# First gate of a two-layer mixture-of-experts kernel: turned input ahead of the rest, row means out of the gate's products, squares on ScalarE

## The reference

```python
x = x + 0.5 * ffn(layernorm(x))      # mixture of 8 experts, top 2 of each row
x = x + attention(layernorm(x))      # 16 heads, causal
x = x + 0.5 * ffn(layernorm(x))      # the same experts again
```

```python
m = mean(x, -1); v = var(x, -1); xn = (x - m) / sqrt(v + 1e-5)
logits = xn @ gate_weight.T                      # (4096, 8)
top_w, top_i = top_k(softmax(logits), 2)         # two experts and weights per row
primary = experts that are the first choice of some row
# experts that are nobody's first choice are rerouted by the similarity matrix
y[e] = (silu(g) * u) @ down[e].T,  g, u = split(xn @ gate_up[e].T)
out  = sum over the two experts of weight * y[e]
```

## Time and profile before

| | |
|---|---|
| time, median of 3 runs (lowest, highest) | 1196.34 us (1195.28, 1199.88) |
| the profiled execution: time, span | 1202.0 us, 1200.3 us |
| the first gate in its span | about 3 to 97.8 us |
| DVE busy over the span | 767.0 us (64%) |
| PE busy over the span | 993.4 us (83%) |
| ACT, POOL busy over the span | 675.0 us (56%), 508.3 us (42%) |

### The profile page before, as it was taken

How to read it: one execution, slowest core, us unless ns; L and a number is a source line. 1 busy time by engine, 2 the same in 40 slices (tenths; PEclk the granted TensorE clock), 3 DMA queues, 4 the chain that set the end, 5 groups by cost and what they waited for, 6 DMA issues and landing times. The chain is left out here.

```text
span 1200.3 us, 25180 instructions
## 1 busy us (share of the span) xinstructions
PE 993.4 (83%) x9046; PEld 722.6 (60%) x9046; DVE 767.0 (64%) x1557; ACT 675.0 (56%) x1595; POOL 508.3 (42%) x692
## 2 busy tenths in 40 slices
PE   5226999999789967999999999999887299999930
PEld 1125788787778854555555555555546178888830
DVE  3995444444377637888888888888617844444437
ACT  2733445444357522777787877878737545555410
POOL 1535667675455540222232323323210067777720
PEclk9757999999579985999999999999969689999975
DMA  8723555553447554345464553544219423333349
GB/s 305 229 97 98 191 196 202 198 182 136 154 135 249 178 157 90 73 106 123 98 148 104 113 119 95 122 103 102 57 45 344 162 84 105 103 102 106 98 140 315
DMA packets 100582, 172.94 MB, mean 144 GB/s; under 512 B 16240, under 2 KB 64368, under 8 KB 100464
## 3 DMA queue, kind: packets, MB, share of 16 engines
q1 hardware_dynamic: 86640, 133.57, 38.9%
q0 software_dynamic: 13824, 37.77, 9.2%
HBM read 101.55 MB, written 69.47 MB: 142 GB/s over the span
## 5 line engine op out<-in xcount | busy, mean ns | idle before, releaser
L1814 ACT ACTIVATE spare<-h_psS 128x512 f32<-128x512 f32 x576 | 306.6, 601 | 92.8 <-PE h_psS L1724 90.5
L1842 DVE TENSOR_REDUCE h_part<-h_psM 128x2 f32<-128x1024 f32 (+3 forms) x256 | 249.1, 1015 | 11.5 <-PE h_psM L1703 10.9
L1877 POOL TENSOR_SCALAR_AFFINE_SELECT spare<-spare 128x256 f32<-128x256 f32 x256 | 99.5, 407 | 303.7 <-ACT spare L1814 303.7
L886 PE MATMUL m_psG<-wgu,m_x_hi 128*128 x576 | 195.0, 420 | 1.2 <-DVE m_x_lo L960 1.2
L864 POOL DMA_INDIRECT ys<-m_y,m_slot_u x144 | 142.3, 988 | 78.4 <-ACT m_y L951 53.5
L1751 PE MATMUL h_psO<-spare,a_VP 128*17 128x256 f32 (+3 forms) x3072 | 167.0, 337 | 8.9 <-ACT spare L1805 8.7
L1703 PE MATMUL h_psM<-h_KT,h_QT 48*128 48x512 f32 (+3 forms) x768 | 146.2, 423 | 22.5 <-DMA h_QT<-a_QD 14.8
L1724 PE MATMUL h_psS<-h_QT,h_KT 49*128 49x512 f32 (+3 forms) x768 | 159.2, 407 | 3.0 <-ACT spare L1814 2.3
L858 POOL DMA_INDIRECT m_xg<-xn,m_slot_u x140 | 135.7, 969 | 47.8 <-issue 22.3
L970 DVE TENSOR_TENSOR m_h<-m_act_g,m_psG 128x256 f32<-128x256 f32 x144 | 60.6, 421 | 136.1 <-ACT m_act_g L944 136.1
L886 PE MATMUL m_psY<-wdn,m_h_hi 128*128 x576 | 128.5, 304 | 10.8 <-issue 6.5
(11 more groups left out here) (230 smaller groups left out, 1570.4 us busy)
## 6 DMA issues: line engine op xcount, KB each, us to landing
xn<-spare SPq DMA_DIRECT2D x16, 512.0 KB, 5.8
wg_d<-wgu SPq DMA_DIRECT2D x16, 512.0 KB
p_yg<-ys SPq DMA_DIRECT2D x16, 512.0 KB, 5.5
a_KD<-spare SPq DMA_DIRECT2D x32, 256.0 KB, 3.0
h_KT<-a_KD SPq DMA_DIRECT2D x64, 128.0 KB
h_QT<-a_QD SPq DMA_DIRECT2D x64, 128.0 KB
a_OD<-spare SPq DMA_DIRECT2D x128, 64.0 KB, 2.5
wgu<-wg_d SPq DMA_DIRECT2D x16, 512.0 KB, 10.5
```

Of the source, the lines that this page charges most:

```text
L886: m = pe.matmul(out, s[:, c, :], ww[:, bass.ds(at + c * width, width)], start=(n == 0), stop=(n == 3 * CC - 1))
L1814: act.activation(prob[k % NP][:, h, :], psS[x % NS][:, :], ACT.Exp).then_inc(s_read, 1)
L1842: m = dve.tensor_reduce(out, psM[k % NM][:, :, at:at + n], AX.X, ALU.max, negate=True)
L1877: m = pool.affine_select(block, block, [[0, 2], [1, P]], ALU.is_ge, 0.0, 0, -1)
```

## The change

1. SP issues all eight `turned(h)` first, then weights and rows by turns, then the similarity matrix, and all stores last, in the order 0, 1, 4, 2, 5, 6, 3, 7.
2. The gate product uses all M = 10 columns of `middle`; columns 8 and 9 hold -1/256, so that column 8 gives minus the mean of each row. `measure` goes. `means(q)` copies that column into SBUF, and ACT gets `square(h)`: four activations that square X plus the negative mean, with the sum over the row as second result. `deviate` reads these sums.
3. Normalised rows: groups 0 to 3 by ACT (two buffers), 4 to 7 by DVE (two buffers). Before it was 0 to 5 and 6 to 7.
4. `low_places` reads a new f32 ramp `iota_f` in place of the bf16 one, and that of batch 0 is cut in halves around `choices(1)`.
5. The lists of ACT and DVE are put in a new order. `ranks(0)` goes from behind group 6 to behind group 7.

```diff
-    W, RA, RB, RT = 4, 3, 1, 4
+    W, RA, RB, RT, M = 4, 2, 2, 4, sh.M
-    BY_ACT, BY_DVE = tuple(range(NH - 2)), (NH - 2, NH - 1)
+    BY_ACT, BY_DVE = tuple(range(NH // 2)), tuple(range(NH // 2, NH))
@@ SP
                 for h in range(NH):
-                    load(h)
                     turned(h)
...
+                for e in (0, 1): weights(e)
+                load(0); load(1)
+                for e in (2, 3): weights(e)
+                load(2); load(3); weights(4); load(4); load(5); weights(5)
+                load(6); load(7); weights(6); weights(7)
                 route.similarities(sp, sim_d)
+                for h in (0, 1, 4, 2, 5, 6, 3, 7):
+                    store(h)
@@ PE
-                        m = pe.matmul(psL[h % 2][0:E, :], middle[:, c, 0:E], xT[h % RT][:, c, :], ...
+                        m = pe.matmul(psL[h % 2][0:M, :], middle[:, c, :], xT[h % RT][:, c, :], ...
-                    if h == NH - 2:
+                    if h == NH - 1:
                         route.ranks(pe, 0)
@@ ACT
+                def square(h):
+                    act.wait_ge(x_in[h], 16)
+                    act.wait_ge(mean_done, route.batch_of(W * h) + 1)
+                    act.wait_ge(centred, 1)
+                    for t in range(W * h, W * h + W):
+                        if t >= 2:
+                            act.wait_ge(squared, t - 1)
+                        act.activation(psM[:, t % 2 * C:t % 2 * C + C], X[:, t, :], ACT.Square, bias=mean[:, t:t + 1],
+                                       accum_out=squares[:, t:t + 1]).then_inc(squared, 1)
...
                 # the new list, shortened to its calls
+                across(0..7); high(0); high(1); square(0); square(1); high(2); high(3); square(2); square(3)
+                deviate(0); high(4); partitions(0..2); normal(0); normal(1); square(4); square(5); high(5)
+                partitions(3); square(6); square(7); deviate(1); high(6); partitions(4); normal(2)
+                partitions(5); high(7); partitions(6); normal(3); partitions(7); exponentials
@@ POOL
+                pool.iota(iota_f[:, :], [[1, P]], 0, 0, ...).then_inc(iota_done, 1)
@@ DVE
-                        dve.bn_stats(stats[:, t, :], X[:, t, :]).then_inc(stat_done, 1)
-                        dve.bn_aggr(mv[:, t, :], stats[:, t, :]).then_inc(var_done, 1)
-                    dve.scalar_tensor_tensor(shift[:, at], mv[:, at, 0], -1.0, rstd[:, at], ...
+                    dve.tensor_tensor(shift[:, at], mean[:, at], rstd[:, at], ALU.mult).then_inc(rs_done, 1)
+                def means(q):
+                    dve.wait_ge(lg_done, route.FROM[q + 1] // W)
+                    dve.tensor_copy(mean[:, route.tiles(q)], scores(q)[:, :, E]).then_inc(mean_done, 1)
...
+                means(0); choices(0); place(0); low_places(0, half 0); means(1); choices(1)
+                low_places(0, half 1); begins; place(1); shift; block_places(0..2); invert(0)
+                low_places(1); block_places(3..5); invert(1); block_places(6); normal(4)
+                block_places(7); normal(5); normal(6); normal(7); open_gap; similar; weights; slots; experts
```

More of the change, by code:

```diff
@@ L605, in _ @@
                 for h in range(NH):
[L606 removed]
                     turned(h)
[L608 to L611, removed]
[L612 to L622 removed]
+                for e in (0, 1):
+                    weights(e)
+                load(0)
+                load(1)
+                for e in (2, 3):
+                    weights(e)
+                load(2)
+                load(3)
+                weights(4)
+                load(4)
+                load(5)
+                weights(5)
+                load(6)
+                load(7)
+                weights(6)
+                weights(7)
+                route.similarities(sp, sim_d)
+                for h in (0, 1, 4, 2, 5, 6, 3, 7):
+                    store(h)
                 for j in range(RA):
@@ L771, in _ @@
                                          gate_w[:, :, :], ALU.mult, ALU.add).then_inc(centred, 1)
-                for h in range(5):
-                    measure(h)
+                means(0)
                 choices(0)
-                invert(0)
-                for h in range(5, NH):
-                    measure(h)
                 route.place(dve, T, 0)
+                dve.wait_ge(iota_done, 1)
+                route.low_places(dve, 0, 0, iota_f)
+                means(1)
                 choices(1)
-                invert(1)
-                normal(BY_DVE[0])
-                route.open_gap(dve, T, rstd[:, :])
-                route.low_places(dve, 0)
+                route.low_places(dve, 0, 1, iota_f)
                 route.begins(dve, T)
@@ L788, in _ @@
                     route.block_places(dve, i)
-                normal(BY_DVE[1])
-                route.low_places(dve, 1)
-                for i in range(3, route.CH):
+                invert(0)
+                route.low_places(dve, 1, None, iota_f)
+                for i in range(3, 6):
                     route.block_places(dve, i)
+                invert(1)
+                route.block_places(dve, 6)
+                normal(4)
+                route.block_places(dve, 7)
+                for h in range(5, NH):
+                    normal(h)
+                route.open_gap(dve, T, rstd[:, :])
+                route.similar(dve, T)
                 route.weights(dve, T)
-                route.similar(dve, T)
                 route.slots(dve, T)
```

89 lines of the change are left out of this document (49 added, 40 removed).

## The result

The changed kernel takes 1205.06 us (median of 20 runs, 1199.24 to 1210.72). The kernel before, run beside it, takes 1200.20 us (median of 20, 1195.28 to 1205.89; the three runs shown ahead of the prediction are among them). The ratio is 1.0035, 95% interval 1.0018 to 1.0051: slower by 0.35% by this ratio, by 4.9 us between the two medians. That is within the half a per cent that the prediction called no change; only the very end of the interval reaches it. Part of the closeness of the total (1.5 us) is therefore luck: two errors of opposite sign. The profiled execution of the changed kernel took 1206.9 us, with a span of 1205.2.

A forecast was written before the change was run, and what follows sets the result against it. DVE, held by POOL's subtractions, was taken to bound the first gate; with ACT's late list and DVE's tail its end moves from 92.4 to 99.7 us, so 1196.34 + 7.3 = 1203.6 us, range 1190 to 1208.5.

The forecast's parts named there:

- The path: First gate: DVE under POOL to the first block matrix at 62.2 us, ACT to 79.05, then DVE to 99.7.
- the held ramp: First half of low_places(0), 16 f32-ramp instructions: held by POOL at 1.2 us each, 0.22 in quiet.
- ACT's wait: At ACT's first partition: from 45.8 us it waits 16 us for DVE's first block matrix at 62.2.
- DVE's wait for the second deviation: After low_places(1): DVE, done long before, waits for ACT's deviate(1), which ends at 79.05 us.
- a store ahead of `normal(7)`: Late on DVE: normal(7) waits until group 5 is stored, 0.15 + 2.9 us, to 92.2.
- the tail: From the second deviation's end on ACT, 79.05 us, through DVE's last matrices, normalisations and slot list, to 99.7.
- D: End of the slot list on DVE, closing the first gate: 92.4 us before, forecast 99.7, +7.3.
- The front: Loads, scores, first choices: DVE picks batch 0 from 21.2 to 25.9 us, group 7 scored 27.3, DVE on at 28.6.
- `place(0)`: DVE's step from 28.6 to 35.0 us: five of seven instructions each end with a POOL instruction; 1.7 without POOL.
- The unheld ramp: Rival, chance 0.25: POOL doesn't hold the f32 ramp, first half takes 4.3 us, D 96.0, total 1199.9.
- Only long runs are held: Rival, chance 0.2: place(0)'s small instructions slip past POOL in 1.8 us; D 86.6, -5.8, total 1190.5.
- The late stores: Rival, chance 0.1 with other length: group 5's store takes 7.8 us or queues; D 104.6, total 1208.5.

The follow-up runs named there:

- squares ahead: Changed kernel with ACT's squares of groups 4 to 7 and the second deviation ahead of its first partition; D 94.67 us against 96.9.
- tail filled: Changed kernel with open_gap and similar moved ahead of the normalisations of group 7, into DVE's store wait; D 93.99 us against 96.9.
- bf16 ramp: Changed kernel with the old bf16 ramp as source of all places, nothing else; D 94.23 us against 96.9.
- choices first: Changed kernel with means(1) and choices(1) ahead of the first half of batch 0's places; D 94.11 us against 96.9.
- rows as before: Changed kernel with six groups normalised by ACT, two by DVE, open_gap and similar ahead of the last group; D 91.24 us against 96.9.
- the last version: Changed kernel with the single edits combined, first of two orders (all squares and second deviation ahead of partitions); D 81.1 us, ratio 0.9919 to the kernel before.

## Why the prediction was right

**The steps that held.** The path, the held ramp, ACT's wait (14.99 us, 16 predicted), DVE's wait for the second deviation, a store ahead of `normal(7)`, and above all the tail: from the end of the second deviation's ACT instruction to D 99.7 - 79.05 = 20.65 us were predicted, and 96.90 - 76.24 = 20.66 measured. Its parts agree as well: `normal(4)` 4.1 predicted and 4.15 measured, `normal(5)` 4.05 and about 4.2, from its end to `normal(7)` 3.1 and about 3.1. The front was right to 0.7 us: choices(0) from 20.9 to 25.4 (21.2 to 25.9), group 7 scored at 26.8 (27.3), DVE going on at 27.99 (28.6). All of this follows the working by which the timelines of before were continued.

**The terms that were mis-sized.** D came 2.8 us earlier than predicted (96.9, not 99.7):

| term | predicted | measured | effect on D |
|---|---|---|---|
| DVE goes on after the ranks | 28.6 | 27.99 | -0.6 |
| `place(0)` | 6.4 | 4.0 | -2.4 |
| first half of the matrices | 13.7 | 14.4 | +0.7 |
| `means(1)`, `choices(1)` | 4.8 | 4.9 | +0.1 |
| second half | 3.5 | 3.2 | -0.3 |
| to ACT's first partition | 5.2 | 5.25 | 0 |
| ACT to the second deviation's end | 16.85 | 16.5 | -0.4 |
| tail | 20.65 | 20.66 | 0 |

One term is far larger than the others: `place(0)`. The working had each of its five one-source instructions end with an instruction of POOL. The trace shows two passing at 0.17 us each: L204 behind L203 and L206 behind L205, pairs in which the second doesn't wait for the first. POOL's next instruction starts at the same moment as L204 (30.56). This is no fixed property of the code. With squares ahead the same seven instructions took 6.4 us, L204 and L206 costing 1.30 us each, though POOL stood as in the changed kernel to 0.02 us (L203 starts 1.34 us after its first subtraction in both, POOL's third subtraction 2.47 and 2.45 us after it). In the four other kernels of that kind (tail filled, bf16 ramp, choices first, rows as before) L204 took 0.17 us. It looks like a tie at the change of turns that went the other way once in six. Timeline of DVE, squares ahead:

```profile
28.64 0.53 DVE L202 CAST m_rank_i<-m_rank 128x32 int32<-128x32 f32 x1
29.19 1.20 DVE L203 TENSOR_SCALAR m_hi_i<-m_rank_i 128x32 int32<-128x32 int32 x1
30.31 1.30 DVE L204 TENSOR_SCALAR m_lo_i<-m_rank_i 128x32 int32<-128x32 int32 x1
31.64 1.19 DVE L205 CAST m_hi<-m_hi_i 128x32 f32<-128x32 int32 x1
32.75 1.30 DVE L206 CAST m_lo<-m_lo_i 128x32 f32<-128x32 int32 x1
34.09 13.39 DVE L216 TENSOR_SCALAR spare<-m_iota_f,m_lo 128x128 bf16<-128x128 f32 x16
```

So the working gave the upper of two values that one and the same list of instructions can show, 4.0 and 6.4. The 2.4 us don't reach D whole, though. When `place(0)` takes them, POOL has that much less left to do behind it: in the one trace that shows it, with squares ahead, the first half took 13.39 us instead of 14.38, and `choices(1)` with `means(1)` 4.6 instead of 5.0. From DVE's going on to the second half it is 24.3 us there, 23.3 in the changed kernel, and 24.9 in the working (53.5 - 28.6). The rows -2.4, +0.7 and +0.1 of the table thus belong together: of their sum of -1.6 us the two ways of `place(0)` are 1.0, and 0.6 are the working's own. With the held `place(0)` D would have come near 97.9, a shift of some +5.5 by this estimate, which is still within half a per cent. The side with the largest of the three chances, "slower by more than half a per cent" at 0.43, didn't come because of that 1.0 us and of several small terms of the same sign (-0.6, -0.6, -0.3, -0.4); "same" had been given 0.42. The range of 1190 to 1208.5 was wide: the kernel before lies in it too.

**The rivals.** The unheld ramp gave +3.6 us, nearer in size than the forecast, and is false all the same: the f32 ramp cost 14.38 us beside POOL and 3.23 without it, and the same 16 in bf16 cost 12.06. A forecast can be nearer for the wrong reason; the row that was named in advance (0.27 or about 1.2 us each between 35 and 48) tells them apart. It showed 1.21 each at first (four in the 4.85 us from 32.01) and 0.21 in POOL's pause (five in the 1.06 us from 42.88), so that the mean of 0.90 is a mixture of the two. "Only long runs are held" asked for a `place(0)` under 2 us, and it took 4.0. The late stores didn't come: `normal(7)` waited 1.80 us.

The Trainium skill, SBUF — State Buffer, section Who interferes with whom, has a Vector instruction with one source through both ports and a GpSimd instruction shut each other out for the other's whole length, by the number of ports alone. The mixed form bears this out (1.21 us each held, 0.20 in quiet), as the int32 instructions of `place` do. In these traces the holding isn't confined to instructions with one source: block matrices, with two, took 1.8 us instead of 0.75 with the squares ahead.

**What stays open.** Why the two instructions pass in one execution and not in another isn't settled: the starts agree to 0.02 us, where the rows resolve 0.01, and no run repeats one kernel's trace to count how often. The tie is a guess; the six traces show only the two outcomes. The gains of the single edits weren't tried in every pairing either, so that the 11.3 us of the last version can't be shared out among them. And of the 1.5 us that POOL costs more than before, no run says which part comes from where POOL's instructions now lie and which from such ties.

## What to carry to other kernels

Where POOL's instructions and DVE's can't run together, count DVE's path as its own work plus the POOL time beside it, see which of DVE's instructions are held at all (here the reductions weren't), and put POOL's work into DVE's waits: that gave 6.4 us here, and taking a wait away that POOL had been using gave 2.0 of 6.4. Work taken off the bounding engine (here all row statistics) is worth only what isn't lost in a new wait behind the list of the engine that takes it over; look in that engine's list for what it now stands behind. When a step's cost depends on whose turn it is, carry both values through the sum, not the higher, and let the steps behind it start when each value says: what one step pays to POOL the next ones don't pay again.

## What the runs showed of the hardware

- A short DVE instruction right behind a held one, not waiting for its end, can pass at 0.17 us or be held for 1.30, with the same code and POOL at the same place to 0.02 us.
- Beside POOL's subtractions the five reductions of `choices` kept their quiet length (0.27 to 0.39 us) in every trace, while its two-source instructions took anything from 0.22 to 1.36 us. With block matrices (two sources) the holding went either way: with the squares ahead they took 1.8 us instead of 0.75, and in the first of the last two kernels one POOL subtraction took 3.23 us instead of 1.26 while three block matrices beside it ran at their quiet length (2.08 us).
- A square with its row sum costs ACT two instructions, 0.45 and 0.18 us, yet they follow one another every 0.49 us for 256 columns; the two of the second gate were 0.51 apart.
- The kernel before took 1272 to 1283 us at some times instead of 1195 to 1206. The record gives the same chip number for one such time (1278.20) and for one of 1194.87, so it can't be laid to one chip. The gate is as long there (the front and the held instructions cost the same to a few hundredths); the difference lies behind it, in code that all these kernels share. From 110 to 346 us, with squares ahead at such a time and in the changed kernel at the other, the single instructions are alike (a matmul of the first expert product 0.420 and 0.417 us, POOL's instruction that stores results 0.987 and 0.988), but POOL's waits for ACT ahead of these stores are longer, 64.8 us in 30 waits against 39.2 in 59. TensorE's granted clock isn't lower there: it is 0.97 against 0.93. The cause wasn't found. It is the reason why only kernels run side by side are compared by their totals.
